# Loading the first feed-forward weight in blocks of four hidden slices instead of two

## The reference, cut to what matters

```python
# layer 0: two residual blocks, x is [8, 4096, 1024]
x = x + layernorm(linear_attention(layernorm(x)))        # q,k = elu+1; kv = k^T v; gate; Wo
x = x + layernorm(ffn(layernorm(x)))

def bit_linear(x, w):          # x rounded to 127 levels per row, w to -1/0/1
    xq = act_quant(x); wq = weight_quant(w)
    return einsum('bsd,hd->bsh', xq, wq)

def ffn(x):
    h = bit_linear(x, w1)                    # 1024 -> 4096
    h = depthwise_conv1d(h, conv_w, conv_b)  # width 3 along the sequence
    return bit_linear(silu(h), w2)           # 4096 -> 1024
```

## Time and profile before

| | us |
|---|---|
| median of 2 runs | 8516.75 (8512.71 to 8520.79) |
| the profiled execution | 8547.53 |
| its slowest core's span (core 2) | 8546.0 |
| the other cores' spans | 8493.3 to 8545.3 |
| TensorE busy, core 2 | 3691.8 (43%) |
| VectorE busy | 2859.8 (33%) |
| ScalarE busy | 1023.6 (12%) |
| mean granted TensorE clock, cores 0 to 7 | 0.723 to 0.733 |
| DMA, mean over the span | 58 GB/s |

### The profile page before, as it was taken

The page is one execution under the profiler, slowest core; times in us unless marked ns, Lnnn a source line. Parts: engine busy times, 40 slices in busy tenths (PEclk is TensorE's granted clock), DMA queues, the critical chain, the costliest instruction groups (busy, mean ns, idle before and its releaser), DMA issues.

```text
span 8546.0 us, 65939 instructions; the slowest of 8 cores (8493.3 to 8546.0 us)
## 1 busy us (share of the span) xinstructions
PE 3691.8 (43%) x20044; PEld 2029.1 (24%) x20044; DVE 2859.8 (33%) x5319; ACT 1023.6 (12%) x1615; POOL 386.8 (5%) x214
## 2 busy tenths in 40 slices
PE   0245556665588888852232232223214223322422
PEld 0122222222355555531110111111012011111200
DVE  4522211112433333323423432332342343234243
ACT  0211111111112112210101001010010100101000
POOL 0100000000000000000000000000000000000000
PEclk9987777777788889876675676666666566666665
DMA  6620000000201101132231132223123113222311
GB/s 189 201 63 20 20 24 21 20 20 15 89 30 38 38 30 35 35 75 55 56 86 54 42 81 62 53 65 77 49 52 86 54 45 79 65 57 59 86 44 44
DMA packets 679993, 495.11 MB, mean 58 GB/s; under 512 B 561891, under 2 KB 561891, under 8 KB 677606
## 3 DMA queue, kind: packets, MB, share of 16 engines
q1 hardware_dynamic: 586470, 289.52, 13.4%
q10 hardware_dynamic: 73728, 134.25, 5.6%
q0 software_dynamic: 19456, 67.12, 2.2%
HBM read 423.71 MB, written 67.11 MB: 57 GB/s over the span
## 4 chain that ended last, share of the span: by engine, by line
PE 33%; DVE 28%; DMA 18%; issue 8%; ACT 7%; POOL 3%; DVEq 2%; ACTq 0%; SPq 0%; POOLq 0%
DMA w2qs<-w2q 8%; DMA w1qs<-w1q 6%; PE pk L520 5%; PE po L825 5%; PE ph L1247 4%; PE pv L520 4%; PE pg L761 4%; POOL H L1134 3%; DVE H L1054 3%; DVE H L1051 3%; PE po2a L1168 3%; ACT H L1060 2%; DVE H L1046 2%; PE po2b L1168 2%; DVE statsA L175 2%
## 5 line engine op out<-in xcount | busy, mean ns | idle before, releaser
L1247 PE MATMUL ph<-xqT,w1qs 128*128 128x256 bf16 x4096 | 589.7, 309 | 363.1 <-DMA w1qs<-w1q 328.5
L1168 PE MATMUL po2a<-w2qs,hqb 128*128 128x512 bf16 x1024 | 405.1, 486 | 769.2 <-DVE hqb L1145 390.4
L1093 PE MATMUL pbcst<-identf,cmaxb 128*128 128x128 f32 x64 | 28.6, 447 | 1483.6 <-DVE cmaxb L1087 1454.2
L1247 PEld LDWEIGHTS ph<-xqT,w1qs 128*128 128x128 bf16 x4096 | 436.8, 110 | 515.8 <-issue 419.3
L1256 DVE TENSOR_TENSOR H<-ph,invB 128x256 f32<-128x256 f32 x512 | 217.6, 425 | 732.0 <-PE ph L1247 731.7
L1168 PE MATMUL po2b<-w2qs,hqb 128*128 128x512 bf16 x1024 | 424.7, 507 | 0.0
L1134 POOL TENSOR_TENSOR H<-H,sc2B 128x8192 f32<-128x8192 f32 x16 | 257.2, 16076 | 3067.1 <-DVEq L109 3067.1
L1188 DVE TENSOR_SCALAR ffnb<-po2a,fac2c 128x1024 f32<-128x1024 f32 x16 | 20.5, 1283 | 1116.3 <-PE po2b L1168 1116.3
L1093 PEld LDWEIGHTS pbcst<-identf,cmaxb 128*128 128x128 f32 x64 | 11.7, 182 | 1501.0 <-issue 1501.0
L1017 PE MATMUL pbcst<-diagb,onesf 128*128 128x128 f32 x64 | 24.5, 487 | 715.9 <-DVE diagb L1013 715.9
L1168 PEld LDWEIGHTS po2a<-w2qs,hqb 128*128 128x128 bf16 x1024 | 71.6, 101 | 1095.9 <-issue 1095.5
(11 more groups left out here) (206 smaller groups left out, 6893.1 us busy)
## 6 DMA issues: line engine op xcount, KB each, us to landing
w1qs<-w1q SPq DMA_DIRECT2D x256, 512.0 KB, 4.6
w2qs<-w2q ACTq DMA_DIRECT2D x512, 256.0 KB, 2.7
qstage<-w SPq DMA_DIRECT2D x64, 512.0 KB, 4.2
qstage<-w SPq DMA_DIRECT2D x16, 2048.0 KB, 9.3
xin<-x SPq DMA_DIRECT2D x32, 512.0 KB, 3.6
xr_b<-x SPq DMA_DIRECT2D x32, 512.0 KB, 4.1
x<-x_b POOLq DMA_DIRECT2D x32, 512.0 KB, 5.0
x2in<-x SPq DMA_DIRECT2D x16, 1024.0 KB, 5.3
```

The costliest lines, as they stand in the source:

```text
L1168: last = t.matmul(out=PO2[tl][:, half * 512:(half + 1) * 512], lhsT=hqb[:, s, tl * 128:(tl + 1) * 128], rhs=w2qs[:, wb, half * 512:(half + ...
L1247: last = t.matmul(out=pb[:, :], lhsT=w1qs[:, (s // 2) % 2, s % 2, c, :], rhs=xqT[:, buf, c, :], start=(c == 0), stop=(c == 7))
```

## The change

A batch of `w1qs` is now four slices, 1 MB, in place of two. Each of the two buffers doubles (8 KB more SBUF per partition in all), there are 8 loads per chunk instead of 16, and the buffer is freed after the fourth slice. The matmuls, their order and the PSUM buffers stay, and so do the runs of 256 bytes.

```diff
-        w1qs = sb3("w1qs", [128, 2, 2, 8, 128], BF16)
+        w1qs = sb3("w1qs", [128, 2, 4, 8, 128], BF16)
@@ emit_w1_load
-                    out=w1qs[:, wb, :, :, :], in_=w1q_d[2 * b:2 * (b + 1)].transpose([2, 0, 1, 3])),
+                    out=w1qs[:, wb, :, :, :], in_=w1q_d[4 * b:4 * (b + 1)].transpose([2, 0, 1, 3])),
@@ for s in range(32)
-                b = s // 2
+                b = s // 4
-                        last = t.matmul(out=pb[:, :], lhsT=w1qs[:, (s // 2) % 2, s % 2, c, :],
+                        last = t.matmul(out=pb[:, :], lhsT=w1qs[:, (s // 4) % 2, s % 4, c, :],
-                if s % 2 == 1:
-                    w1qs_free[(s // 2) % 2].freed_by((s_hmm, s_hmm.v))
-                    if b + 2 < 16:
+                if s % 4 == 3:
+                    w1qs_free[(s // 4) % 2].freed_by((s_hmm, s_hmm.v))
+                    if b + 2 < 8:
                         emit_w1_load(b + 2)
```

## The result

| | before | changed |
|---|---|---|
| median of the runs (us) | 8550.7 (10 runs) | 8468.4 (11 runs) |
| ratio, with its 95% interval | 1 | 0.9887 (0.9856 to 0.9917) |
| spans by core in the profiled execution | 8493.3 to 8546.0 | 8376.3 to 8466.8 |
| mean span of the eight cores | 8523.8 | 8406.3 |

The change made the kernel faster by 1.1%, about half of the forecast 2.3%, and 8468 lies above the range. (Further runs of the kernel before were taken beside it, so its median is not the one that stood ahead of the prediction.) The ratio is taken over the runs in which no group of cores was held at a lower clock, so it is not the ratio of the two medians. By the ratio, 0.9887 of the 8516.75 that the forecast started from is 8420, and that too is above the range.

The account below looks back on a forecast made before the run. The prediction took the W1 stage's round trip of `w1qs` load and batch as the bound: stages of 46 us instead of 58.5, 16 x 12.5 = 200 us off 8547.5, carried to the run median as 8317 us, range 8260 to 8410.

Parts of the forecast that it names:

- What bounds the stage: W1 stage: the round trip of load and batch sets the cycle; 12.5 us saved per stage comes off the span.
- Matmuls of a batch: W1 stage: 32 matmuls instead of 16 take 3.84 us at full clock, 5.3 to 5.4 us at half-clock price.
- charge of 0.9 us per cycle: W1 stage: allowance for clock falls and late loads, 2.7 us per stage; bounds 0.3 and 1.6 per cycle.
- wait computed for the new cycle: TensorE in the W1 stage: waits 2.9 us per cycle, 3.4 before batch 2; a clock fall costs 1.6 us.
- The load: W1 stage: a 1 MB `w1qs` load takes 4.6 + 2.3 = 6.9 us.
- bounds that I kept: Load of `w1qs`: at least 6.3 us (fastest load, cheaper increment), at most 9.2 us (twice the median).
- shared transfer engines: W1 stage: two loads need 9.4 us of full transfer engines, under the 11.15 us cycle, so the round trip decides.
- rival B: W1 stage: transfer engines become the bound at half of 220 GB/s, stage unchanged, about 8517 us; chance 0.05.
- head of the chunk: Start of each chunk: the two preloads land later, at 5612 and 5616.4, covered by layer norm; nothing charged.
- three signs: Prediction wrong if a load lands after over 8 us, half-clock runs open every batch, or another stage grows.
- A: W1 stage: the long load costs much more, 9.2 us, stage 53.0 us, saving 88 us, 8428 us; chance 0.14.
- C: W1 stage: load issue held, load starts late, 16.2 us, stage 71 us, 200 us slower, 8716 us; chance 0.04.

Follow-up runs that it names:

- split run: Changed kernel with each 1 MB batch brought by two 512 KB loads, first matmul waiting for both: W1 stages sum to 784 us against 817, mean span 8335 us.

## Why the prediction was wrong

*What bounds the stage: right.* The round trip of a load and its batch set the cycle before and after; that the stage's saving comes straight off the span is confirmed (116.6 and 117.4). That the two agree to a microsecond is partly luck, since shifts of 14 and 12 us elsewhere cancelled.

*Matmuls of a batch: wrong, one of the two terms that failed.* The step "Matmuls of a batch: 32 instead of 16, twice 1.92 = 3.84 us at full clock", with a charge of 0.9 us per cycle for falls of the clock and late loads, came out at 5.33 us in nearly every cycle (5.49 on average), 0.75 us more than term and charge together, or 36 us over the 48 cycles of a core. The wait computed for the new cycle, 2.9 to 3.4 us, lay between one after which the clock held and one after which it had fallen, and I took the middle. For such a wait that was no bad reading of the kernel before, where 52 of 151 waits of 2.9 to 3.4 us were followed by a fall, but the two waits that I read do not bound it: one of 2.35 us in the same chunk was followed by a fall. The wait became 4.1 to 4.6 us, and the clock fell to 0.50 in all but one of the 384 such batches. The working had subtracted 4.4 us from the load's 7.3 for the other buffer's batch and a short wait ahead of it. That short wait vanishes once the even batch starts slowly, so the subtraction is 3.7, and the wait 3.6 us even with the load that I had assumed. A slow start thus lengthens the next wait: with the split load (7.15 us) the waits were still 4.1 to 4.5 us and the batches behind them still slow, as the rows of that run show. The runs with extra matmuls price it: 40 to 43 us.

*The load: mis-sized, the other.* "Another 512 KB on a queue that is already moving costs 2.2 us" was read where two loads stood behind a third transfer. A load that starts alone costs 2.7 us more per additional 512 KB (two loads) and 3.3 in one load, so it took 7.7 us in the median, not 6.9 (7.84 on average, which over 48 cycles is 45 us). The split run prices the form at 32 us. Which of the two terms is the larger error is not settled: 36 and 45 us by the terms, 40 and 32 by the runs. The fit that the prediction quoted from the Trainium skill (DMA: Bandwidth & Descriptors, Anatomy of one DMA), made for the other issuing path, would have been further off (1.2 us for the second half megabyte, against 3.3 measured). The bounds that I kept (6.3 to 9.2) held the median; the range for the stage didn't, because its upper end let both terms be a little off, but not both fully.

*The shared transfer engines: right.* They did not become the bound (0.60 busy in the stage, not the 0.7 forecast), and the stage did not stay at 58 us as rival B had it. With four loads under way they reached 0.83 and the stage fell further. Within a load, though, they are full, here in the middle of the one of batch 2, so a load's length is not all round trip:

```profile
5596.00:5601.00 5.00, 2.13 (x19) 1.43 (x16) 1.35 (x4) 0.00 (x0) 0.00 (x0) 1.00 0.98 210
```

*The head of the chunk: right.* The two preloads land far ahead of the first matmul (5588.94):

```profile
L1229 SPq DMA_DIRECT2D w1qs<-w1q x2: 674/2948/5223, 5559.7 to 5560.8; - x2
...
DMA to landing us min/median/max: 9.3/11.1/12.8
```

The last is 5560.8 + 12.8 = 5573.6, with 15 us to spare as forecast. Counted from the issue of `x2in` (5559.08 here, 5601.95 in the earlier trace rows) the two land after 9.9 and 14.5 us, and the forecast's 5612 and 5616.4 are 10.1 and 14.5. The second issue is held for 5.2 us, and nothing stands behind it.

*The signs.* Of the three signs that the prediction named for being wrong, two came: a landing over 8 us (8.6 in the median of all loads) and a half-clock run at the start of every batch behind a wait. The third, another stage that grows, did not. TensorE's wait for the loads is 219 us where about 180 was forecast.

*The rivals.* A gave 53 us for the stage and 8428; it held that a long load costs more than the increment says. That was so, at 7.7 us instead of its 9.2, and the clock brought the rest, so the result lies nearest to A (51 us) by its sum and by neither mechanism alone. I gave A 0.14. That a rise of HBM latency under load, which the Trainium skill names (DMA: Bandwidth & Descriptors, Latency and other measured facts), is part of it was not shown here: splitting a load in two took 0.55 us off and runs of 2 KB took 2.0 off, both with the same bytes in flight. C, a load held at its issue, did not occur within a stage: a second load's issue took 1.2 us in the median and 3.8 at most, and it landed 8.7 us after it began, as a load queued behind another would.

*The probabilities.* Under the 2% bound the change counts as no clear difference, to which I had given 0.28.

## What to carry to other kernels

With two buffers, a larger load halves the number of round trips but lengthens each one; the same memory in more, smaller buffers removes them. Before enlarging a load, price it from loads that start alone, and ask what the longer wait does to TensorE's clock: if the wait falls between one after which the clock held and one after which it did not, take both ends into the range in full, and read more than one wait of each length, since the same length can go either way. The general advice to make loads of 1 MiB or more (Trainium skill, DMA: Bandwidth & Descriptors, Rules for kernel authors) is for rate; here four buffers of half that size moved 163 GB/s in the stage and the two of 1 MB 123.

## What the runs showed of the hardware that was not expected

- One load of 4096 runs of 256 bytes was issued with an added MOVE_SHAPE, took 0.67 us to issue instead of 0.36 and moved larger packets, and landed 0.5 us later than two loads of half the size issued one behind the other. Which of these three makes the 0.5 us was not separated. With 512 runs of 2 KB the MOVE_SHAPE and the longer issue were gone.
- Runs of 2 KB instead of 256 bytes took a lone load of 512 KB from 4.4 to 3.5 us, and one of 1 MB from 7.7 to 5.7.
- The stretch ahead of the first W1 stage, which no edit touches, took 3729 us in the kernel before and 3910 in the run with extra matmuls in the changed kernel (core 2; 3894 to 3915 over the eight), with a mean granted clock of 0.76 against 0.83. In the run with extra matmuls in the kernel before two cores had it too (0 and 1: 3848 and 3842 at 0.78 and 0.79, the other six 3720 to 3735 at 0.83). The first 1800 us are the same. Behind them the granted clock stands at 0.81, neither of the two usual levels, for 1.4 to 1.6 ms of the stretch on each of the eight cores of that run, and never in the kernel before; TensorE's busy time for the same work grows from 1428 to 1653 us there (core 2). In the changed kernel cores 2 to 5 had this level for 0.12 to 0.31 ms, which goes with its stretch being 14 us longer. What sets it no trace shows. It does not show in the stage sums: the run's cores with 11 and 15 us of it in their W1 stages sum to 777 and 782 us, the one with 186 us to 781. The stretch is a larger difference than any effect of the change, which is why the experiments were read by their stages.

The rows of that stretch, before (up to 3728.9) and the run with extra matmuls (up to 3900, and one piece of it):

```profile
0.00:3728.90 3728.90, 2273.94 (x13472) 1328.27 (x13472) 1146.61 (x1959) 617.71 (x823) 111.50 (x166) 0.83 0.17 52
```

```profile
0.00:3900.00 3900.00, 2499.10 (x13462) 1418.56 (x13462) 1141.82 (x1945) 616.30 (x821) 111.31 (x166) 0.76 0.16 50
...
2455.00:2495.00 40.00, 39.26 (x306) 31.99 (x304) 12.11 (x29) 7.15 (x14) 0.00 (x0) 0.81 0.00 1
```
